# Causal zeros of two score units set on GpSimd instead of by mask products on TensorE

## What is computed

```
def _L0_attn_b_ref(x, Wqkv, bqkv, Wproj, bproj):
    B, T, C = x.shape
    n_head = 16
    hd = C // n_head
    x_proj = x @ Wqkv + bqkv
    q = x_proj[:, :, :C].reshape(B, n_head, T, hd)
    ...
    att = jnp.einsum('bhtd,bhsd->bhts', q, k) * (1.0 / jnp.sqrt(jnp.float32(hd)))
    causal = jnp.tril(jnp.ones((T, T), dtype=bool))
    att = jnp.where(causal, att, jnp.float32(-jnp.inf))
    att = jax.nn.softmax(att, axis=-1)
    y = att @ v
    ...
```

## Time and profile before

| | |
|---|---|
| median of 3 runs | 3762.95 us (3755.66 to 3763.63) |
| profiled execution | 3763.16 us, span 3761.3 us |
| attention | about 1000 to 3145 us of the span |
| TensorE, VectorE, ScalarE, GpSimd busy | 95%, 79%, 58%, 44% |
| mask products (L1951) | 2560 |
| exponentials (L1862) | 2304 of 601 ns |
| granted TensorE clock | 0.978 of full speed over the span |

### The profile page before, as it was taken

How to read it: one execution, slowest core, us unless ns; L and a number is a source line. 1 busy time by engine, 2 the same in 40 slices (tenths; PEclk the granted TensorE clock), 3 DMA queues, 4 the chain that set the end, 5 groups by cost and what they waited for, 6 DMA issues and landing times. The chain is left out here.

```text
span 3761.3 us, 76026 instructions
## 1 busy us (share of the span) xinstructions
PE 3560.0 (95%) x25550; PEld 2347.9 (62%) x25550; DVE 2952.9 (79%) x9275; ACT 2183.7 (58%) x4151; POOL 1666.4 (44%) x2027
## 2 busy tenths in 40 slices
PE   6999899999689999999999999999999998999997
PEld 5888666666455665566656656655666555666664
DVE  8998666766688888888888888888888893676775
ACT  1110456655337766766676667667667665656654
POOL 2332123223345556656555565565565511223323
PEclk9999899999879999999999999999999999999999
DMA  2333112111497978787887879788887832121211
GB/s 74 100 98 109 57 46 68 54 59 35 116 140 111 126 115 129 120 127 123 122 127 119 132 116 126 116 119 123 124 134 121 120 41 80 40 68 46 68 46 45
DMA packets 694291, 361.16 MB, mean 96 GB/s; under 512 B 297905, under 2 KB 660913, under 8 KB 693937
## 3 DMA queue, kind: packets, MB, share of 16 engines
q1 hardware_dynamic: 693936, 356.62, 53.5%
HBM read 204.49 MB, written 150.99 MB: 95 GB/s over the span
## 5 line engine op out<-in xcount | busy, mean ns | idle before, releaser
L1862 ACT ACTIVATE att_probs<-att_s 128x512 f32<-128x512 f32 x2304 | 1212.5, 601 | 461.2 <-PE att_s L2001 234.4
L1737 DVE CUSTOM_DVE_ANT_0 att_s<-att_s,att_above 128x384 f32<-128x384 f32 (+3 forms) x2048 | 950.2, 519 | 132.8 <-PE att_s L1981 127.1
L1981 PE MATMUL att_s<-att_ks,att_qs 48*128 48x512 f32 (+3 forms) x3072 | 896.0, 401 | 5.7 <-DVE att_maxima L1740 3.6
L2001 PE MATMUL att_s<-att_qs,att_ks 49*128 49x512 f32 (+3 forms) x3072 | 852.4, 373 | 20.5 <-DVE att_maxima L1737 5.2
L2001 PEld LDWEIGHTS att_s<-att_qs,att_ks 49*128 49x128 f32 x3072 | 487.6, 186 | 464.0 <-ACT att_probs L1862 271.6
L1740 DVE TENSOR_REDUCE att_maxima<-att_s 128x1 f32<-128x512 f32 x1024 | 661.9, 684 | 98.3 <-PE att_s L1981 93.2
L2029 PE MATMUL att_o_ps<-att_probs,att_vs 128*32 128x512 f32 (+3 forms) x6144 | 620.5, 497 | 25.1 <-ACT att_probs L1862 22.1
L1981 PEld LDWEIGHTS att_s<-att_ks,att_qs 48*128 48x128 f32 x3072 | 485.9, 189 | 26.4 <-DVE att_maxima L1737 8.9
L1097 PE MATMUL ffn_h2p<-ffn_h,ffn_w 128*128 128x512 f32 x768 | 365.0, 598 | 3.0 <-ACT ffn_h L968 0.9
L1951 PE MATMUL att_s<-att_mask,att_places 64*128 64x128 bf16 (+1 forms) x2560 | 327.7, 212 | 0.0
L1737 DVE DVE_READ_ACCUMULATOR2_ANT att_maxima<- 128x1 f32 x2048 | 293.0, 143 | 0.0
(11 more groups left out here) (292 smaller groups left out, 6384.8 us busy)
## 6 DMA issues: line engine op xcount, KB each, us to landing
att_staged<-qk_scratch SPq DMA_DIRECT2D x768, 128.0 KB, 7.6
qk_scratch<-att_parts SPq DMA_DIRECT2D x128, 512.0 KB, 3.4
ffn_x<-x SPq DMA_DIRECT2D x64, 512.0 KB, 5.2
ssm_x<-in_L_attn_a_x_dram SPq DMA_DIRECT2D x32, 512.0 KB, 3.7
x<-ssm_y SPq DMA_DIRECT2D x32, 512.0 KB, 3.0
x<-ffn_y SPq DMA_DIRECT2D x32, 512.0 KB, 2.9
att_x<-x SPq DMA_DIRECT2D x32, 512.0 KB, 7.4
v_scratch<-att_v_tok SPq DMA_DIRECT2D x32, 512.0 KB, 5.3
```

Of the source, the lines that this page charges most:

```text
L1737: last = v.tensor_tensor_reduce(scores, scores, above[:, CH - w:CH], 1.0, -3.0e38, ALU.add, ALU.max, to)
L1862: a(probs[u % PROBS][2 * g + p][:, 0:n], bank[:, 0:n], ACT.Exp).then_inc(exp_done, 1)
L1981: last = mm(bank[:, col:col + w], rows_of(qs[buf], g, KROWS, p, BT * blk, BT * (blk + 1)), rows_of(ks[buf], g, KROWS, p, t0, t1), start=k ...
L2001: last = mm(bank[:, col:col + w], rows_of(ks[buf], g, SHIFT + 1, p, BT * j, BT * (j + 1)), rows_of(qs[buf], g, SHIFT + 1, p, t0, t1), star ...
```

## The change

The diff, without three spots of moved code and the lists of semaphore names:

```diff
+    SELECTED = ((7, 8), (7, 8), (), (7, 8))
-    PROBS = 3
+    PROBS, KEPT_BEHIND = 3, 1.4
-    NORMALISE_AT = (14.4, 15.5, 16.5, 17.5)
+    NORMALISE_AT, NORMALISE_EARLY_AT = (14.4, 15.5, 16.5, 17.5), (12.4, 13.3, 14.1, 14.9)
...
+        def kept_before(quad, u):
+
+            of = [4 * len(units) for units in SELECTED]
+            units = SELECTED[quad % 4]
+            return sum(of) * (quad // 4) + sum(of[:quad % 4]) + (4 * units.index(u) if u in units else 0)
...
+        def blocks_at(bank, cols):
+
+            at = slice(cols[0] // P, cols[-1] // P + 1, max(1, (cols[-1] - cols[0]) // P))
+            return bank.rearrange("p (n w) -> p n w", w=P)[:, at, :]
...
+                def keep_causal(quad, step, g):
+
+                    u, p = step // 2, step % 2
+                    pool.wait_ge(exp_done, 2 * STEPS * quad + 2 * step + g + 1)
+                    cols = diagonals(PASS2[u], False)
+                    m = blocks_at(probs[u % PROBS][2 * g + p][:, :], cols)
+                    nc.gpsimd.affine_select(out=m, in_=m, pattern=[[0, len(cols)], [1, P]], compare_op=ALU.is_ge, fill=0.0,
+                                            base=0, channel_multiplier=-1).then_inc(causal_kept, 1)
...
-                    if q == 3 and more:
-                        tasks += [(17.5, lambda r=r: bias(b, r)) for r in range(2)]
+                    if q == 0 and not first:
+                        tasks += [(2, lambda r=r: bias(b - 1, r)) for r in range(2)]
...
-                        tasks += [(NORMALISE_AT[0], lambda: rstds(hb))]
-                        tasks += [(NORMALISE_AT[t], lambda t=t: normalise(hb, s, t)) for t in range(TT)]
+                        at = NORMALISE_EARLY_AT if q == 0 else NORMALISE_AT
+                        tasks += [(at[0], lambda: rstds(hb))]
+                        tasks += [(at[t], lambda t=t: normalise(hb, s, t)) for t in range(TT)]
+                    for of, units, ahead in ((quad - 1, SELECTED[(q - 1) % 4], STEPS), (quad, SELECTED[q], 0)):
+                        for step, group in itertools.product((2 * u + p for u in units for p in range(2)), range(2)):
+                            at = step + group / 2 + KEPT_BEHIND - ahead
+                            if of >= 0 and (at >= 0 if ahead else at < STEPS):
+                                tasks += [(at, lambda of=of, step=step, group=group: keep_causal(of, step, group))]
...
-                              stop=k == len(PASS2[u]) - 1 and not diagonals(PASS2[u], False))
+                              stop=k == len(PASS2[u]) - 1 and (u in SELECTED[buf] or not diagonals(PASS2[u], False)))
...
-                        if diagonals(PASS2[u], False):
+                        if diagonals(PASS2[u], False) and u not in SELECTED[buf]:
...
-                    pe.wait_ge(exp_done, 2 * STEPS * quad + 4 * u + 4)
+                    if u in SELECTED[q]:
+                        pe.wait_ge(causal_kept, kept_before(quad, u) + 4)
+                    else:
+                        pe.wait_ge(exp_done, 2 * STEPS * quad + 4 * u + 4)
```

More of the change, by code:

```diff
@@ L4 @@
 from contextlib import ExitStack
+import itertools
 import numpy as np
@@ L1668, in _ @@
                 run(pool, sequence)
+                for step, group in itertools.product((2 * u + p for u in SELECTED[3] for p in range(2)), range(2)):
+                    if step + group / 2 + KEPT_BEHIND >= STEPS:
+                        keep_causal(4 * NB - 1, step, group)
                 for r in range(4):
```

20 lines of the change are left out of this document (10 added, 10 removed).

## The result

The changed kernel takes 3777.75 us (median of 5, 3771.09 to 3787.53) beside 3759.18 us (3755.66 to 3763.63) for the kernel before on the same chip: ratio **1.0045**, 95% interval 1.0031 to 1.0058 (the two medians by themselves give 1.0049). The forecast was 3765 us and "no change" was the likeliest case; the time lies inside the range, near its upper end. The profiled execution of the changed kernel took 3777.75 us (span 3775.6), against 3763.16 (3761.3) before.

What follows compares the result with a forecast made beforehand. TensorE, busy 95% of the span, was taken as the bound. Quads 3 and 0 (+2.9 us), quad 1 (+2.2) and ends without such tasks (-3.3) gave +1.9 on 3763.2: 3765 us, range 3746 to 3779.

Steps and rivals of the forecast that it cites:

- The waits, their places and their cause: times_v waits for selects behind GpSimd's splits: 0.8 us before unit 7 (quad 1), 1.1 before unit 8 (quad 3).
- Unmasked, I give both 1.0: Parts 10 and 11, masked 1.23 and 1.28 us, were each to take 1.0 without masks, saving 0.25 each.
- 0.65 us per changed quad: Masks' saving in parts 9, 10 and 11 together; 31 us over 48 quads if GpSimd is always in time.
- The sum over a batch: Net change of one batch's attention: +0.21 us for quads 3 and 0 together, +0.15 for quad 1.
- Quad 0's wait behind the residual's load: Unit 8's selects 2 to 4 stand behind residual 2's bias, which awaits its load; TensorE waits 0 to 1.5 us.
- it moves with the split, 0.65 earlier: Residual 2's load in quad 0 hangs on projection 5's split through a fixed-length chain, so lands 0.65 us earlier.
- DMA, ACT and VectorE get no new work: Closing assumption of the sum: the change adds nothing to these queues, so no term was given for them.
- GpSimd is later: Slower rival: transfers, not split 5, set residual 2's load in quad 0; 3772 us, 3778 with dearer selects; chance 0.27.
- Locked out by VectorE: Slower rival: VectorE holds ports GpSimd's selects need, up to 2 us each; 10 give 3785 us; chance 0.03.
- All in time: Faster rival: GpSimd's selects are never last, so 48 quads save 31 us, giving 3732 us; chance 0.07.
- The wait is given back: Partly faster rival: VectorE catches up while TensorE waits, shrinking later waits by 17 us, giving 3748; chance 0.15.

Runs made afterwards that it cites:

- the kernel with both: Changed kernel with the masks kept on TensorE and GpSimd's selects also made and waited for; ratio 1.0041 to the kernel before.
- the moves alone: Changed kernel with all masks on TensorE and no selects, only the normalisation and two biases moved on GpSimd; ratio 0.9990 to the kernel before.

## Why the prediction was partly right: point by point

- **The waits, their places and their cause: right.** Line 1993 fell to 1792 products, and unit 8 after quad 3 and unit 7 after quad 1 wait behind splits 5 and 2. The sizes were forecast too large, 1.1 and 0.8 for 0.82 and 0.23 us, and the total 35 for 20 us. Part of that is prices: two blocks of 128 columns take 0.385 us from start to start (0.77 for two), not 0.45, which is nearer the first of the two estimates by the Trainium skill (GPSIMD Engine Reference, section 7, Performance pitfalls for Q7 kernels: 0.41) than the second; and the signal 0.05 (2132.46 to 2132.51), not 0.1. The rest is the next point: TensorE comes later to the place of the wait than forecast.
- **"Unmasked, I give both 1.0": wrong in quads 1 and 3, and the mis-sized term.** Part 10 came to 0.95 everywhere and part 11 to 0.95 in quad 0; but part 11 takes 1.39 in quads 1 and 3, bound by VectorE. The first part of quad 1 also grew, from 1.18 to 1.46 us, and part 9 shrank by the 0.15 forecast only in quad 3, by 0.05 in quads 0 and 1. The forecast saw VectorE as the bound of part 9 and asked only there. 0.65 us per changed quad, 1.95 per batch, measured 0.76 (undisturbed batch 128.52 before, 127.76 without masks and selects; 127.76 is the sum of 32.14, 31.50, 30.96 and 33.16, the lower fifths). The ceiling was 12 us, not 31.
- **The sum over a batch: right by two errors that cancel.** Forecast +0.36 us; measured 128.85 - 128.52 = +0.33, made of -0.76 of gain and some +1.0 of waits (129.55 - 128.55, the kernel with both against the moves alone). Sixteen batches of it are 5 us. That this term came out is luck.
- **Quad 0's wait behind the residual's load: in the changed kernel absent, as a mechanism shown.** The step "it moves with the split, 0.65 earlier" counted the earlier start of the chain but let quad 0 end at nearly its old place; the 0.9 us by which the wait before it delays quad 0 is what covers the load. With that wait removed it appeared: 2.05 us in the rows shown.
- **"DMA, ACT and VectorE get no new work": true, and the step that failed.** Nothing in the sum allowed for TensorE's own instruction stream. Removing 48 weight loads and 48 matmuls from a batch changed 9.3 packets per batch to 9.0, so that their places move little from batch to batch, and five quads 3 in a row got a late packet in the stretch with full queues. Long quads 3 lose 19.7 us instead of 9.0, +10.7. With the 5 us above that makes 16, where the two profiled executions are 14.6 apart (17.8 in the attention, 3.5 less outside it; the other quads' own long ones, some 8 and 11 us, are in neither term). That the time still lies inside the range is luck in part: the same kernel again took 3785.59 us, above the range's 3779, beside 3765.26.
- **The rivals.** "GpSimd is later" gave 3772, close to the measured time, for a reason that is not the one. "Locked out by VectorE": the longest of 384 selects took 423 ns, so no; the rule of the Trainium skill (SBUF — State Buffer, section SBUF: two separate sides) was not seen to act on them, and no run tried it. "All in time": without any wait still 0.9986, so its 3732 rested on the mis-sized term. "The wait is given back": in the opposite sense, since it is the masks' time that VectorE kept.

## What to carry to other kernels

When work is cut from the engine that sets the pace, ask at every place of the cut which engine comes next there, with its own rows, not once for the whole. In-order queues turn a small new task into a wait when it stands behind a task that hangs on the waiting engine itself; put it ahead, and look at once for the next task in the queue that waits for a transfer. And if "issue" idle time grows in one place of a long unrolled loop, compare instruction packets per iteration and the transfers that run there: a count near a whole number can repeat a collision over many iterations, and a shift of half a packet in front of the loop shows whether that is the cause.

## What the runs showed of the hardware that was not expected

- TensorE stops for 0.6 to 4 us, without a wait in its program, where an instruction packet (16 KB by the view of the queues: 138 packets, 2.26 MB) moves late among data transfers that fill the queues to 97.6%: 17 to 25 us behind the packet before it, where one in 14 us is the mean. Half a packet of harmless instructions in front was worth 0.4 to 0.6% of the changed kernel, and nothing of the kernel before.
- After 3.92 us without work the granted clock was 0.50 (1.2 GHz) over the next 3 us, 0.70 over the next 5, and 1.00 after that.
- A select of 128 columns on GpSimd takes 283 ns or more and one of two blocks of 128 up to 423; in a row they follow each other every 0.28 to 0.30 and 0.385 us. Between a select's end and the matmul that waits for it pass 0.05 us.
